# Query-row loads of a two-layer graph attention kernel begun by SyncE instead of ScalarE

## The reference, cut to what matters

```python
# layer 0: 4 heads of 32; edge attributes are added to keys and values
kj = k[src] + e
alpha = jnp.einsum('ehc,ehc->eh', q[dst], kj) * scale
amax = jax.ops.segment_max(alpha, dst, num_segments=n)
expa = jnp.exp(alpha - amax[dst])
asum = jax.ops.segment_sum(expa, dst, num_segments=n)
msg = (v[src] + e) * (expa / (asum[dst] + 1e-16))[..., None]
out = jax.ops.segment_sum(msg, dst, num_segments=n)
# layer 1: one head of 256; a weight per edge is added to the score
scores = jnp.sum(q[dst] * k[src], axis=-1) * scale + (edge_weight[:, None] @ we + be)[:, 0]
out = jax.ops.segment_sum(v[src] * softmax_by_dst(scores)[:, None], dst, num_segments=n)
x = layer_norm(x + out + linear(x, ws, bs), g1, b1)   # then a feed-forward part and a norm
```

## Time and profile before

| | before |
|---|---|
| runs, median (lowest to highest) | 5072.7 us (5072.0 to 5076.51) |
| the profiled execution: span from first to last instruction | 6753.4 us |
| TensorE busy / weight loads | 4299.6 us (64%) / 3492.8 us (52%) |
| VectorE busy | 3831.3 us (57%) |
| ScalarE busy | 3003.4 us (44%) |
| POOL busy | 3308.1 us (49%) |
| edge phase of layer 0, by the trace | about 127 to 3135 us |
| edge phase of layer 1, by the trace | about 3422 to 6400 us |

### The profile page before, as it was taken

The page is one execution under the profiler, slowest core; times in us unless marked ns, Lnnn a source line. Parts: engine busy times, 40 slices in busy tenths (PEclk is TensorE's granted clock), DMA queues, the critical chain, the costliest instruction groups (busy, mean ns, idle before and its releaser), DMA issues.

```text
span 6753.4 us, 105844 instructions
## 1 busy us (share of the span) xinstructions
PE 4299.6 (64%) x23291; PEld 3492.8 (52%) x23291; DVE 3831.3 (57%) x12902; ACT 3003.4 (44%) x6997; POOL 3308.1 (49%) x3637
## 2 busy tenths in 40 slices
PE   6555555565565566566746666666666666666698
PEld 3454554555455555454534555555554555554587
DVE  4565665666566666666734444455454444444588
ACT  1444454555454454554324444444444444444432
POOL 2545555455555455452355545554555554454355
PEclk8777777777777777777978778787888787777899
DMA  6555555555555555553446556565666665555422
GB/s 201 148 145 148 146 145 146 145 153 148 149 152 145 145 152 154 148 148 99 122 141 163 161 153 162 157 162 157 164 160 158 160 160 158 157 163 158 125 73 70
DMA packets 774181, 996.11 MB, mean 147 GB/s; under 512 B 189569, under 2 KB 559489, under 8 KB 773553
## 3 DMA queue, kind: packets, MB, share of 16 engines
q10 hardware_dynamic: 394272, 443.81, 23.8%
q0 software_dynamic: 150224, 410.39, 22.7%
q1 hardware_dynamic: 229056, 135.14, 7.5%
HBM read 862.98 MB, written 125.90 MB: 146 GB/s over the span
## 4 chain that ended last, share of the span: by engine, by line
another core or an unknown queue 22%; PE 21%; DVE 17%; issue 16%; DVEq 7%; ACTq 5%; ACT 5%; DMA 2%; POOL 2%; SPq 1%; POOLq 1%
PE ps L1377 20%; DVE rows L1009 2%; DVE score L1021 2%; DVE prod L1033 2%; ACT oh L750 2%; DVE acc L1174 2%; DMA acc_d<-acc 2%; ACT place L738 1%; ACTq L827 1%; DVE prod L1016 1%; DVEq L1233 1%; ACTq L730 1%; SPq L266 1%; DVEq L1231 1%
## 5 line engine op out<-in xcount | busy, mean ns | idle before, releaser
L637 POOL DMA_INDIRECT rows<-kv_d,src_all x1564 | 1535.2, 982 | 1543.1 <-DVE score L1021 951.0
L637 POOL DMA_INDIRECT rows<-x_d,src_all x1564 | 1487.0, 951 | 1450.5 <-DVE prod L1033 962.3
L1377 PE MATMUL ps<-place 128*128 128x256 bf16 (+2 forms) x10560 | 1459.9, 288 | 296.4 <-issue 186.8
L1377 PEld LDWEIGHTS ps<-place 128*128 128x128 bf16 (+1 forms) x10560 | 1250.9, 149 | 587.4 <-issue 317.6
L1377 PE MATMUL ps<-rows,oh 128*128 x3520 | 1093.2, 470 | 457.3 <-DVE oh L1154 340.7
L1033 DVE SCALAR_TENSOR_TENSOR prod<-rows,ps 128x256 f32<-128x256 f32 x1760 | 637.3, 418 | 906.8 <-remote 549.9
L1377 PEld LDWEIGHTS ps<-rows,oh 128*128 128x128 f32 x3520 | 797.8, 236 | 617.9 <-issue 478.8
L750 ACT ACTIVATE oh<-iota_row,rel 128x128 f32<-128x128 f32 x2640 | 837.9, 388 | 552.9 <-remote 408.8
L1377 PE MATMUL ps<-msg,oh 128*128 128x132 f32 x3520 | 607.0, 330 | 595.8 <-DVE msg L1149 331.8
L1377 PEld LDWEIGHTS ps<-msg,oh 128*128 128x128 f32 x3520 | 544.1, 235 | 638.9 <-DVE msg L1149 421.0
L738 ACT ACTIVATE place<-dst_row,node_tab 128x512 f32<-128x512 int32 (+1 forms) x880 | 613.2, 708 | 385.4 <-DVE acc L1174 145.3
(11 more groups left out here) (217 smaller groups left out, 4152.9 us busy)
## 6 DMA issues: line engine op xcount, KB each, us to landing
dst_row<-in_dst_row ACTq DMA_DIRECT2D x880, 256.0 KB
place<-q_d ACTq DMA_DIRECT2D x440, 192.8 KB
acc_d<-acc ACTq DMA_DIRECT2D x440, 128.5 KB
ea<-in_ea SPq DMA_DIRECT2D x440, 128.0 KB
acc_d<-acc ACTq DMA_DIRECT2D x440, 66.0 KB
place<-q_d ACTq DMA_DIRECT2D x440, 64.0 KB
rows<-kv_d,src_all POOLq DMA_INDIRECT x1564
rows<-x_d,src_all POOLq DMA_INDIRECT x1564
```

The lines of the kernel that those rows point to most:

```text
L637: pool.indirect_dma_start(out=L.rows[:, t % SLOTS, j, 0:D], out_offset=None, in_=L.table, in_offset=bass.IndirectOffsetOnAxis(ap=src_all[: ...
L1377: return pe.matmul(out_, lhsT=lhsT, rhs=rhs, start=first, stop=last)
```

## The change

SyncE begins the loads of query rows in both layers, in load_pair, and reads block_tab itself, for four pairs at a time. Its load_ahead waits for s["q"] in layer 1 too, not only in layer 0. ScalarE loses the load, its wait and its reading of block_tab. The buffers, their number, the bytes and the value waited for (pair g - 4's queries made) stay the same.

```diff
@@ SyncE, edge_loads @@
-                landing, edges_of, idx_steps = {}, {}, {}
+                landing, edges_of, block_of, idx_steps = {}, {}, {}, {}
...
                 def load_pair(g, par, st):
...
+                    if g % 4 == 0:
+                        block_of.update(zip(range(g, g + 4), load_row(ENGINE.SP, block_tab[0:1, g:g + 4])))
+                    sp.dma_start(L.qw[place], window(L.q_d, block_of.pop(g))).then_inc(s["ld_q"][place], 16)
                     if L is L0:
...
                 def load_ahead(c, par, st):
 
                     g = CH * c + st
-                    wait(s["q"], g - 1) if L is L0 else None
+                    wait(s["q"], g - 1)
                     load_pair(g + 2, (par + (st + 2) // CH) % 2, (st + 2) % CH)
@@ ScalarE, edge @@
-                step_of, block_of = {}, {}
+                step_of = {}
...
-                    if g % 4 == 0:
-                        block_of.update(zip(range(g, g + 4), load_row(ENGINE.Activation, block_tab[0:1, g:g + 4])))
-                    wait(s["q"], g - PLACES + 1)
-                    act.dma_start(L.qw[g % PLACES], window(L.q_d, block_of.pop(g))).then_inc(s["ld_q"][g % PLACES], 16)
```

## The result

The changed kernel takes 4908.97 us (median of 4 runs, 4903.95 to 4916.29), the kernel before 5074.6 us on the same chip: ratio 0.967, 95% interval 0.965 to 0.968, 166 us faster. The forecast of 4999 us had the sign right and less than half of the size. The time is that of the second rival, 4909 us; the experiments show that the reason it gave was not the one at work.

The account below looks back on a forecast made before the run. Waits were taken to bound the kernel, with ScalarE among layer 1's pace-setters and VectorE holding layer 0's path. Issues and reads gave -77 us, other terms 0; x 0.963 = -74, so 5072.7 - 74 = 4999 us, range 4905 to 5095.

Parts of the forecast that it names:

- second rival: Layer 1: without its wait ScalarE runs a pair ahead, freeing TensorE and VectorE; -164 us, 4909 us, chance 0.10.
- The mechanism: On ScalarE: losing 880 issues of 0.51 us and 220 block_tab reads of 0.31 us shortens the chain.
- that term: ScalarE's issues and reads on the path: 100 + 15 = 115 us at most, 77 us taken.
- factor of two thirds: On ScalarE's issues and reads: two thirds of the 115 us upper end taken, 77 us; lower end 0.
- held-up records: Profile of the kernel before: writing records held up execution; 22% unnamed chain removed, the rest scaled by 0.963.
- The lost wait: ScalarE before the weighing, waiting for TensorE's queries: worth 0 to 146 us, taken as 0.
- POOL's floor: Layer 1: four gathers per step, 5.0 us, 391 steps make 1955 us; at most 243 us to be had.
- SyncE's side: SyncE gains 880 issues, 220 reads and a layer 1 wait: price 0 to 220 us, taken as 0.
- The rival's mechanism: SyncE's word on landed rows comes late and VectorE stands; 5210 us or 5126 us, chance 0.12.
- Transfers: Query rows' 113 MB move from ScalarE's queue to SyncE's: between -74 and +20 us, taken as 0.
- The cover takes it all: ScalarE's saved issue time becomes waits for sums or VectorE's additions: 5073 us within 10 us, chance 0.16.
- The profiled span: Profiled execution of the changed kernel: same number of records, so span near 6750 us, within 1%.

Follow-up runs that it names:

- e13: Changed kernel with 880 issues of 16 partitions of window 0 put back on ScalarE, one pair late, no table reads: ratio 0.9925.
- e3: Kernel before, ScalarE loading only 16 of 128 query-row partitions, one pair later, SyncE the other 112, two pairs ahead: ratio 0.9979.
- e8: Kernel before, ScalarE loading window 0's query rows for every pair, without the 220 block_tab reads: ratio 0.9915.
- e1: Changed kernel with ScalarE's wait for the queries of pair g - 4 put back, nothing issued behind it: ratio 0.9684.
- e2: Kernel before, ScalarE's load of query rows and its wait moved one pair later: ratio 1.0004.
- a1: Changed kernel run again, no edit: ratio 0.9687, 4923.6 us beside 5076.2 us.
- b0: Kernel before, unchanged, profiled a second time: ratio 0.9999, 5102.5 us, profiled span 5105.8 us.
- e7: Kernel before with the change made in layer 1 alone, layer 0 as before: ratio 0.9841.
- a2: Changed kernel again, on a chip where the kernel before takes 6672.5 us: ratio 0.9978.
- e9: Changed kernel with SyncE also taking ScalarE's dst_row loads and step_tab reads, four pairs ahead: ratio 0.9991.
- e4: Changed kernel with ScalarE again reading block_tab every four pairs, 220 reads whose values nothing uses: ratio 0.9671.
- e6: Changed kernel with four semaphores for the stores of sums, one per acc buffer, instead of two: ratio 0.9676.
- e10: Changed kernel with LEAD = 6 instead of 5, so POOL may gather one step further ahead: ratio 0.9674.
- e5: Kernel before, each query-row load begun in two halves of 64 partitions, 880 issues more on ScalarE: ratio 1.1015.

## Why the prediction was right and wrong

**The mechanism was right.** Issue time on ScalarE is the gain: 121 to 131 us for the 880 issues (e13) and 27 to 43 us for the 220 reads (e3 against e13; e8). Together that is 148 to 174 us, which takes in the 166 us. The waits (e1, e2) and the bytes (e3) leave nothing large beside them, and TensorE's clock does not either: a1 had the gain at 0.900, b0's clock was 0.901.

**The step that failed is the size of that term**, above all in layer 0: "since VectorE holds that layer's path I take 12". Two thirds of layer 0's part, reads included, is 12 us; layer 0 was half of the gain, some 87 us (166 - 79, e7). In layer 1 the same working gives 62 us, and 79 were measured (e7). Of the 92 us that the forecast lacks, 75 are layer 0's. Some pieces do look like the earlier trace rows, but in b0's chain of the whole layer ScalarE and its queue have over 34% and VectorE's named lines about 12%.

Both shares of L730 were read in a profile whose execution took 6753 us. I subtracted the unnamed 22% of its chain and took the rest for the real kernel, since the remainder came within 4% of the median. The sum was near, its parts were not: ScalarE's lines had 10% there and 29% in b0. Where the execution is that long, the other engines are held up, and what ScalarE saves turns into waits for them; a2 shows this, with the change worth 0.2% and the idle time before the one-hot tiles 368 us above the first profile's. With L730's shares from b0 the same working gives 163 x 0.51 / 0.41 = 203 us and 398 / 4 x 0.31 = 31 us of reads, two thirds of which are 156 us. That factor of two thirds was a choice between 0 and all, not a reading; that it fits here (166 / 234 = 0.71) is luck.

**The reason given for the held-up records does not hold alone.** "I take it that the execution was held up while its records were written": b0, the same program with as many records, has a span of 5105.8 us, and on two chips every run took over 6.6 ms. That the first profile's execution was of that kind is likely (span, clock and chain are alike) but not shown. What holds such executions up stays open; a lower granted clock goes with it (0.79 to 0.80 against 0.90), but the slow records of SyncE are not TensorE's.

**The lost wait**: 0, as taken (e1, e2). The rival that had the right time had it for this wait, so it falls, and its hit is luck; it was right only that layer 1 comes near POOL's floor (about 2050 us by the changed kernel's trace, against 1955).

**SyncE's side**: 0, as taken; VectorE's waits for its word are 75 us in all. The rival's mechanism exists, and appears when SyncE's waits are on ScalarE and first nodes (e9), not with a wait on queries.

**Transfers**: about 13 us of gain (e3 against e2), against 0 taken and -74 as the end. The rule of the Trainium skill (DMA: Bandwidth & Descriptors, "Issuing engines are not separate DMA queues"), that another issuing engine saves only the time to begin the transfer, agrees with e3_thin here. That this time is usually small beside the transfer is no comfort: 880 issues made 2.4 to 2.6% of the kernel's time (e13).

**The cover takes it all**: no. But something else does set the pace right behind: the changed kernel does not react to 220 reads more (e4), to freer stores (e6) or to a further step for POOL (e10).

**The profiled span** was forecast at 6750 us and came at 4905.9: the length of the first one was not the records' doing alone.

## What to carry to other kernels

A DMA issued by an engine that also computes costs its compute units time as soon as two issues stand in a row, here 0.31 us for the second. Moving the second to an idle queue is worth a part of its time while that engine sets the pace: here 121 to 131 us of 880 x 0.51 = 449 us, as the next path was close behind. And it is worth that only if the waits that come with it are met early, since all that stands behind them in the new queue waits too. Before shares of a chain are turned into microseconds, compare the profiled span with the timed runs: if it is a third longer, take another profile; subtracting the unexplained part does not give back the shares of the rest.

## What the runs showed of the hardware that was not expected

- The same program took 5073 to 5103 us on most chips and 6665 to 6673 us on two others, with granted clocks of 0.90 and 0.80. Which engine is the limit differs between the two: the change is worth 3.3% on the one kind and 0.2% (0.0 to 0.4) on the other. The cause was not found.
- A DMA issue from ScalarE took 0.487 us for 64 partitions, 0.339 us for 128 and 0.338 us for 16 (e5, b0, e3). In these three, time to issue does not follow the number of bytes or rows; each is the median of its kind in one profile. Issues from a fixed address took 0.445 us for 128 partitions (e8) and 0.442 us for 16 (e13), without the 0.066 us of register steps of a computed one.
